# A streaming cross-attention whose running maximum is renewed every two chunks instead of every four, with a shorter lag

## The reference, cut to what matters

```
ctx: (1, 12544, 256), x: (1, 128, 256), H = 16, DH = 16
q = split_heads(x_q @ Wq + bq) * dp_scale
k = split_heads(x_kv @ Wk + bk)
v = split_heads(x_kv @ Wv + bv)
attn = einsum('bhic,bhjc->bhij', q, k)      # L0: causal, L1: masked, L3: q partly rotated
o = einsum('bhic', softmax(attn), v)
x = x + o @ Wo + bo
```

## Time and profile before

| what | value |
|---|---|
| three runs | 1980.28, 1974.17, 1979.61 us; median 1979.61 |
| profiled execution | 1976.85 us, span 1975.0 |
| mean granted clock of PE | 0.901 |
| busy over the span: PE | 1678.7 us (85%) |
| DVE, ACT, POOL | 1031.8 (52%), 934.6 (47%), 740.2 us (37%) |
| L0, L1, L3: ramp | 48.5, 57.4, 56.5 us |
| mixed steps (42 each) | 365.5, 375.6, 367.2 us |
| tail | 62.1, 66.0, 58.4 us |

### The profile page before, as it was taken

How to read it: one execution, slowest core, us unless ns; L and a number is a source line. 1 busy time by engine, 2 the same in 40 slices (tenths; PEclk the granted TensorE clock), 3 DMA queues, 4 the chain that set the end, 5 groups by cost and what they waited for, 6 DMA issues and landing times. The chain is left out here.

```text
span 1975.0 us, 46123 instructions
## 1 busy us (share of the span) xinstructions
PE 1678.7 (85%) x18939; PEld 1385.3 (70%) x18945; DVE 1031.8 (52%) x1383; ACT 934.6 (47%) x1754; POOL 740.2 (37%) x652
## 2 busy tenths in 40 slices
PE   5899999998636999999998659896169999999974
PEld 4788888876515788888886449775158888888752
DVE  6655557871336766666662330003575555565413
ACT  1566766764100456565654213101016667667642
POOL 8655555520007555555530000000275555555102
PEclk9999999998666999999997869897579999999986
DMA  4555555542004555554443018680144555544330
GB/s 138 133 137 138 135 131 123 122 93 58 27 19 106 141 150 153 148 142 135 135 105 83 26 54 288 242 281 33 61 108 119 123 123 122 123 124 116 87 104 3
DMA packets 149860, 231.60 MB, mean 117 GB/s; under 512 B 25112, under 2 KB 67732, under 8 KB 148884
## 3 DMA queue, kind: packets, MB, share of 16 engines
q1 hardware_dynamic: 140388, 220.78, 41.2%
q10 hardware_dynamic: 9264, 7.87, 1.5%
HBM read 107.32 MB, written 0.23 MB: 54 GB/s over the span
## 5 line engine op out<-in xcount | busy, mean ns | idle before, releaser
L1126 DVE TENSOR_REDUCE L_xattn_maxima<-L_xattn_ps 128x2 f32<-128x1024 f32 x600 | 693.4, 1197 | 461.3 <-PE L_xattn_ps L775 451.1
L903 ACT ACTIVATE L_xattn_p_ring<-L_xattn_ps 128x512 f32<-128x512 f32 x1176 | 676.5, 596 | 364.2 <-PE L_xattn_ps L807 339.6
L807 PE MATMUL L_xattn_ps<-L_xattn_q_packed,L_xattn_k_packed 128*128 128x256 f32 x2352 | 512.2, 310 | 39.6 <-ACT L_xattn_p_ring L903 28.7
L807 PEld LDWEIGHTS L_xattn_ps<-L_xattn_q_packed,L_xattn_k_packed 128*128 128x128 f32 x2352 | 354.3, 193 | 156.4 <-issue 93.3
L843 PE MATMUL L_xattn_ps<-L_xattn_p_ring,L_xattn_v_ring 128*17 128x128 f32 x9408 | 299.9, 282 | 2.9 <-DVE L_xattn_ps L1152 2.9
L1025 POOL TENSOR_TENSOR L_xattn_k_ring<-L_xattn_k_full,consts 128x512 fp32r<-128x512 f32 x147 | 155.5, 1058 | 382.8 <-DMA L_xattn_k_packed<-L_xattn_k_ring 182.8
L843 PEld LDWEIGHTS L_xattn_ps<-L_xattn_p_ring,L_xattn_v_ring 128*17 128x17 f32 x9408 | 253.1, 100 | 46.5 <-issue 35.6
L743 PE MATMUL L_xattn_ps<-L_xattn_ctx_halves,L_xattn_w_halves 128*128 128x256 f32 x1764 | 266.4, 291 | 16.5 <-DVE L_xattn_w_halves L1189 11.4
L747 PE MATMUL L_xattn_ps<-L_xattn_w_halves,L_xattn_ctx_halves 128*128 128x256 f32 x1764 | 267.2, 291 | 15.3 <-DVE L_xattn_k_full L1164 10.2
L743 PEld LDWEIGHTS L_xattn_ps<-L_xattn_ctx_halves,L_xattn_w_halves 128*128 128x128 f32 x1764 | 238.9, 197 | 23.0 <-DVE L_xattn_w_halves L1189 12.6
L747 PEld LDWEIGHTS L_xattn_ps<-L_xattn_w_halves,L_xattn_ctx_halves 128*128 128x128 f32 x1764 | 239.0, 197 | 22.0 <-DVE L_xattn_k_full L1164 12.9
(11 more groups left out here) (341 smaller groups left out, 1144.8 us busy)
## 6 DMA issues: line engine op xcount, KB each, us to landing
L_xattn_k_packed<-L_xattn_k_ring SPq DMA_DIRECT2D x588, 128.0 KB, 2.4
...
```

Of the source, the lines that this page charges most:

```text
L807: last = pe.matmul(L.ps[:, bank, d * 2 * S:(d + 1) * 2 * S], self.k_packed[s][:, quarter, d, half * P:(half + 1) * P], q[:, 2 * pair:2 * p ...
L903: act.activation(self.p[t % P_RING][:, 4 * quarter:4 * quarter + 4, :], L.ps[:, E_BANKS[unit % 2], :].rearrange("p (h n) -> p h n", n=S), ...
L1126: dve.tensor_reduce(out[:, d, 2 * v:2 * v + 2, k], L.ps[:, M_BANK + 2 * v:M_BANK + 2 * v + 2, 0:n], AX_X, ALU.max).then_inc(L["batch_reduc ...
```

## The change

- `BLOCK` is 2 instead of 4, and `LAG` 5 instead of 7. There are 25 blocks instead of 13 and 55 steps instead of 57: 5 in the ramp, 44 mixed, 6 in the tail. The rings are 6 and 7 chunks.
- The factor is computed in fp32r: `update_shift` writes the difference as a high and a low part (7 instructions instead of 5), and four matmuls over 32 rows instead of 16 spread it.
- The shift's DMA is issued by SP (`load_shift`, behind `pack_keys`), no longer by ACT.
- `pack_queries` is issued by ACT, a quarter (4 DMAs) at the end of each of four steps from step 1, no longer by SP.
- The tails of the packed tensors are filled by four DMAs on SP (`fill_tails`), in L1 ahead of the mask's load, no longer by POOL.
- The third copy of the queries is made by ACT from the first, no longer by DVE.
- Values of the first 4 chunks (`V_APART`) are projected into the second E bank, since no units use it yet.
- ACT drains the values behind unit 6, no longer behind unit 5.
- In the tail PE has an order of its own: the halves of the attend stand apart, between units 1 and 2 and behind batch 0.

```diff
-LAG = 7
-BLOCK = 4
+BLOCK = 2
+LAG = BLOCK + 3
-K_RING, V_RING, P_RING = 8, 9, 3
+K_RING, V_RING, P_RING = LAG + 1, LAG + 2, 3
+V_APART = LAG - 1
...
-    return min(4 * b + 6, 2 * GROUPS + 2)
+    return min(BLOCK * b + LAG - 1, 2 * GROUPS + 2)
...
+    def load_shift(self, sp, b):
+        sp.wait_ge(L["e_drained"], E_AT["turned", b] + 1)
+        sp.dma_start(self.q_packed[b % 2][96:98, :, :].bitcast(F32), self.stage_T[32:64, :].bitcast(F32))\
+          .then_inc(L["shift_loaded"], 16)
...
         for step in range(STEPS):
-            m = step - LAG + 1
+            m, b = step - LAG + 1, block_turned(step)
+            if 0 <= m < NCHUNK:
+                for quarter in range(4):
+                    self.pack_keys(sp, m, quarter)
+            if b is not None:
+                self.load_shift(sp, b)
             if step + 3 < NCHUNK:
                 self.load_context(sp, step + 3)
-            if step == 1:
-                self.pack_queries(sp)
             self.weight_parts(sp, step)
...
-                             self.net.spread[:, 4 * i:4 * i + 4, :].rearrange("p h n -> p (h n)"), self.stage_T[0:H, :],
-                             start=True, stop=True, skip_group_check=True)
+                             self.net.spread[:, 4 * i:4 * i + 4, :].rearrange("p h n -> p (h n)"),
+                             self.stage_T[0:2 * H, :], start=True, stop=True, skip_group_check=True)
...
+            else:
+                self.pe_unit(pe, m, 0)
+                self.pe_unit(pe, m, 1)
+                self.pe_attend(pe, m - 1, 0)
+                self.pe_unit(pe, m, 2)
+                if b is not None:
+                    self.pe_turned(pe, b)
+                self.pe_unit(pe, m, 3)
+                self.pe_batch(pe, step, 0)
+                self.pe_attend(pe, m - 1, 1)
...
-            self.act_drain_v(act, step)
             if b:
                 self.act_factor(act, b)
             self.act_unit(act, m, 6)
+            self.act_drain_v(act, step)
             self.act_unit(act, m, 7)
+            if 0 <= step - (LAG - 4) < 4:
+                self.pack_queries(act, step - (LAG - 4))
...
-        pool.wait_ge(L["ctx_split"], 2)
-        for c in range(2):
-            pool.memset(self.q_packed[c][tail, :, :].bitcast(F32), 0.0).then_inc(L["q_packed_cleared"], 1)
...
-            last = dve.tensor_tensor(stage[:, 0:H], self.shift[:, b % 2, :], self.shift[:, 1 - b % 2, :], ALU.subtract)
+            delta = self.shift[:, 2, :]
+            o.after(dve.tensor_tensor(delta, self.shift[:, b % 2, :], self.shift[:, 1 - b % 2, :], ALU.subtract))
+            o.after(dve.tensor_copy(stage[:, 0:H].bitcast(F32R), delta))
+            last = dve.tensor_tensor(stage[:, H:2 * H], delta, stage[:, 0:H], ALU.subtract)
```

More of the change, by code:

```diff
@@ L537, in e_order @@
         m = step - LAG
-        b = next((b for b in range(BLOCKS) if turn_step(b) == step), None)
+        b = block_turned(step)
         for u in range(8):
@@ new lines, in fill_tails @@
+    def fill_tails(self, sp):
+        L, tail = self.L, slice(96, P)
+        for c in range(2):
+            sp.dma_start(self.q_packed[c][tail, :, :].bitcast(F32), times(self.net.const("fill")[tail, :], H))\
+              .then_inc(L["tails_filled"], 16)
+        for c in range(2):
+            sp.dma_start(self.k_packed[c][tail, :, :, :].rearrange("p q d t -> p (q d t)")
+                         .rearrange("p (a n) -> p a n", n=P).bitcast(F32), times(self.net.const("ones")[tail, :], H))\
+              .then_inc(L["tails_filled"], 16)
@@ L688, in sync @@
             self.load_context(sp, n)
+        self.fill_tails(sp)
         if self.masked:
@@ L1213, in vector @@
         for step in range(STEPS):
-            b = next((b for b in range(BLOCKS) if turn_step(b) == step + 1), None)
+            b = block_turned(step + 1)
             self.masked_keys(dve, step)
```

152 lines of the change are left out of this document (78 added, 74 removed).

## The result

The changed kernel takes 2083.11 us (median of four runs, 2079.99 to 2089.68) against 1979.4 for the kernel before (median of four): 1.0534 times as long, 95% interval 1.0502 to 1.0567. The forecast was 2035, with a range of 1995 to 2085. The direction was right, and so was the mechanism in the mixed stretches; in the tails it was not. The loss is nearly twice the one forecast: 104 us by the medians, where 56 were expected. 1.0534 times 1979.4 is 2085.1, at the very end of the range, and the interval of the ratio reaches beyond it. (All ratios here leave out one execution of experiment 3's kernel, which took 5022.11 us where the nine others took 1966.84 to 1977.40; nothing on record explains it.)

A forecast was written before the change was run, and what follows sets the result against it. PE was taken to bound the mixed stretches, with ramps and tails chains of waits. Mixed stretches +158.1, ramps −46.6 and tails −55 sum to +56.5 us on the profiled 1976.85, forecast as 2035 us, range 1995 to 2085.

The forecast's parts named there:

- the mixed stretches: Steps of L0, L1 and L3 where projection and scoring run together: 1108.3 us before, 1266.4 forecast, +158.1.
- The new wait: PE idles 1.43 us at each block's attend, as DVE's seven update operations precede the rescale; bounds 0 and some 0.3 more.
- Rivals A: The wait at the attend is covered, 66 × 1.43 = 94.4 us fall away, total 1941; chance 0.10.
- D: Most of a block's 1.03 us beside the wait is covered by PE's idling; some 1975 us likely; chance 0.04.
- The rest of a block: A block step's extra cost in the mixed stretches apart from the wait: 1.83 − 0.60 − 0.20 = 1.03 us.
- the factor: PE's factor in a block step: four F32R matmuls take 0.48 us instead of 1.08, so −0.60; range 0.24 to 1.08.
- the DMA: Shift's DMA issued by SP, no longer ACT: 0.20 us off each block, bounds 0 and 0.62.
- the drain: ACT's V drain behind unit 6 instead of unit 5: 0.6 us of work moves, taken at nothing in plain steps.
- Rival B: The F32R factor is no cheaper, 1.08 us instead of 0.48: +40 us, total 2075; chance 0.12.
- Ramps: Steps before each layer's first unit: −49.6 us for fewer steps and shorter waits, +3 for fills before L1's mask; together −46.6.
- Tails: Steps after each layer's last projection: two fewer give −46.6 us, the new order −8.4; together −55, bounds −35 and −65.
- rival C: PE's clock falls in the mixed stretches: at 0.95 in all three up to +63 us, total 2098; chance 0.12.

The follow-up runs named there:

- experiment 3: Changed kernel with DVE's rescale ahead of the update and PE's tail steps in the old order: 1969.73 us, 0.9964 of the kernel before.
- Experiment 1: Changed kernel with one edit, DVE's rescale ahead of the update at the end of a step: 1984.52 us, 1.0052 of the kernel before.
- Experiment 6: Kernel of experiment 3 with ACT issuing the queries' four packing quarters after steps 1, 2, 2 and 3: 1956.22 us, 0.9902 of the kernel before.
- experiments 2: Changed kernel with one edit, PE's tail steps in the old order: 2067.41 us, 1.0452 of the kernel before.
- experiment 5: Kernel of experiment 3 with L0's weight-preparing operations moved between DVE's two reductions of a step: 1963.88 us, 0.9931 of the kernel before.

## Why the prediction was right in its cause and wrong in its size

- **The new wait** was forecast at 1.43 us and is 1.45 (1.39 idle). It occurs 21 times in a layer's mixed stretch, not 22, as the first block is never rescaled. Rivals A and D are out: the margin of the earlier trace rows was as thin as it looked. Experiment 1 shows the cause.
- **The rest of a block** was forecast at 1.03 us and is 9.52 − 8.28 = 1.24. Its parts: the factor takes 221.70 − 221.11 = 0.59, not 0.48, so 0.49 off the former 1.08 (the 0.12 us of a matmul twice as wide was no upper bound); the DMA gives 0.35 and not 0.20; the drain costs 0.25 and not nothing. 1.83 − 0.49 − 0.35 + 0.25 = 1.24. Rival B (0.60 more per factor) is out. The estimate by the Trainium skill ("TensorE: Matmul & The Clock Gate", section "Back-to-back issue gap"), 0.32 us for the four, was farther off than the row: a matmul took 0.15 here. 0.21 in 66 blocks is 14 us; less the three waits that don't occur, 4, that makes 10 of the table's 11.5.
- **Ramps**: two steps less, as forecast. The total is off by 4.3 us only because errors cancel: L0 is 3.8 longer than forecast, L1 3.0 shorter, L3 3.5 longer. (The prediction's "about 47" for L0's ramp is a slip; its sum gives 48.5 − 14.6 = 33.9, and 37.7 was measured.) What it left out is what ends the ramp next: the last quarter of the queries, issued by ACT behind step 4's values, 4.7 to 5.6 us of idle in front of unit 0. Experiment 6 shows it. Two waits that it took off didn't go as told. In L0 PE still waits 3.69 us for POOL's `k_ring` in front of the first batch (3.97 before), though the fills are gone from POOL. In L3 the wait of 6.46 for POOL is gone (it stood at a later batch, not at the first), but PE now waits 7.20 for ACT's keys, since ACT makes the third copy of the queries (L1015) ahead of them and waits for DVE's first:

```profile
1513.85 1.91 ACT L1015 ACTIVATE L_xattn_p_ring<-L_xattn_q_hi 128x2048 f32<-128x2048 f32 x1 [6.65 <-DVE L_xattn_q_hi L1249]
...
1516.64 2.90 PE L771 MATMUL L_xattn_ps<-L_xattn_ctx_halves,L_xattn_w_halves 128*128 128x256 f32 x12 [7.20 <-ACT L_xattn_k_full L964]
```

No run moves that copy, so what it costs is open.
- **Tails, the step that failed.** The forecast took 55 us off (two steps less 46.6, the new order 8.4; two fifths of 20 would be 8.0), and 17.6 were measured. I wrote "The wait for the rescale in the tail stays in some form" and put it into the sum at nothing new. Three block starts lie in each tail, and PE waits for the rescale at two of them, 1.45 to 3.11 us each, 14.7 in all where it was 2.9. I had the reason in hand: between batch 1 and the attend the new order leaves three units, the old one four and a batch. I counted that order as a gain of 8.4, for filling gaps, and didn't ask what it brings forward. By experiment 1, taking the update out of the way is worth 24 us in the tails (168.9 to 144.9), and by 3, the old order another 16 (128.9). So the order that was to give 8.4 costs 16, and the wait at nothing costs 24.
- **Clock** (rival C): nothing in the mixed stretches, where it stays at 1.00 with PE 92% busy. It is low in the tails, and there it more than doubles what the waits cost: in experiments 2 and 3 the busy time of the same matmuls goes from 138.9 to 126.6 and 113.7 us, which is 25 of the 40 us that the tails gain from the changed kernel to experiment 3. That was in the forecast only as a remark. What exactly makes the clock fall in one tail and not in another wasn't settled; experiment 5's tails differ by 5 us from 3's although their code differs in L0 alone, and the difference lies in L1 and L3.
